# Two places for the turned probabilities of a background attention, and its output product moved behind the state's own products

## The reference

```python
x = x + _L0_ffn_ref(_layernorm(x), ...)      # causal attention, 16 heads of 64, then a mixture of 8 experts
x = x + _L1_xcond_ref(_layernorm(x), ctx_1024, cond_1024, ...)
# _L0_ffn_ref
q, k = l2norm(q) * q_scale, l2norm(k) * k_scale
logits = where(causal, einsum('bhid,bhjd->bhij', q, k) * 10, -1e9)
out = einsum('bhij,bhjd->bhid', softmax(logits), v).reshape(B, S, H * DH) @ Wo
h = layernorm(out, ln_g, ln_b)
# gate = softmax(h @ gate_w + gate_b); moe = sum over experts of gate * (gelu(h @ w1 + b1) @ w2 + b2)
# _L1_xcond_ref: 512 steps over the tokens
def step(h, x_t):
    attn = softmax(enc_hiddens . (h @ W))          # 77 keys
    context = attn . enc_hiddens
    # z, r, candidate of a GRU from [x_t, context] and h
    return z * h + (1 - z) * cand
```

## Time and profile before

| | us |
|---|---|
| median of 3 runs | 3392.69 (3389.45 to 3431.45) |
| profiled execution, its own time | 3399.51 |
| span of the profile | 3397.6 |
| mean granted TensorE clock | 0.937 of full |
| TensorE busy | 2864.2 (84%) |
| VectorE busy | 2216.0 (65%) |
| ScalarE busy | 1736.5 (51%) |
| GpSimd busy | 883.5 (26%) |

### The profile page before, as it was taken

The page is one execution under the profiler, slowest core; times in us unless marked ns, Lnnn a source line. Parts: engine busy times, 40 slices in busy tenths (PEclk is TensorE's granted clock), DMA queues, the critical chain, the costliest instruction groups (busy, mean ns, idle before and its releaser), DMA issues. The chain is left out here.

```text
span 3397.6 us, 132510 instructions
## 1 busy us (share of the span) xinstructions
PE 2864.2 (84%) x54702; PEld 1897.3 (56%) x54702; DVE 2216.0 (65%) x8486; ACT 1736.5 (51%) x5855; POOL 883.5 (26%) x1882
## 2 busy tenths in 40 slices
PE   5999999776987888898888899899989877777678
PEld 3666666653554454465454566566656544444478
DVE  4666666754426656677566677777768766666665
ACT  3666666433633444475555476666657433333222
POOL 0000000210002444254555344655535200000000
PEclk8999999987888878899899999999999999999879
DMA  4000000000010000010000000000000000000001
GB/s 130 4 5 7 5 4 4 1 10 9 16 51 9 9 9 27 3 40 4 9 9 27 4 28 16 7 10 10 25 10 28 4 3 3 3 4 3 2 32 32
DMA packets 35640, 52.45 MB, mean 15 GB/s; under 512 B 5406, under 2 KB 22760, under 8 KB 34920
## 3 DMA queue, kind: packets, MB, share of 16 engines
q1 hardware_dynamic: 34280, 41.54, 3.9%
q0 software_dynamic: 768, 2.52, 0.3%
HBM read 40.48 MB, written 3.57 MB: 13 GB/s over the span
## 5 line engine op out<-in xcount | busy, mean ns | idle before, releaser
L2010 POOL TENSOR_TENSOR gru_terms<-gru_states,gru_signs 128x8 f32<-128x8 f32 x512 | 103.5, 202 | 1573.7 <-DVE gru_states L2216 1245.0
L1931 ACT ACTIVATE gru_p<-gru_ps_sg,gru_negmax 128x78 f32<-128x78 f32 x512 | 166.9, 326 | 379.1 <-DVE gru_negmax L2185 374.0
L1774 PE MATMUL gru_ps_sg<-score_w,gru_states 128*4 128x78 f32 x4096 | 168.3, 237 | 194.7 <-DVE gru_states L2216 194.5
L1935 ACT ACTIVATE gru_th_r<-gru_pre_r 128x32 f32<-128x32 f32 x512 | 118.4, 231 | 398.6 <-DVE gru_pre_r L2196 398.6
L1572 PE MATMUL gru_ps_sg<-ctx_gate_w,gru_p_t 128*4 128x64 f32 x12288 | 281.1, 228 | 0.0
L342 ACT ACTIVATE self_probs<-self_sc,self_negmax 128x512 f32<-128x512 f32 x256 | 174.2, 684 | 166.2 <-DVE self_negmax L396 166.2
L1987 POOL TENSOR_SCALAR bg_probs<-bg_probs,bg_arsum 128x256 f32<-128x256 f32 (+2 forms) x192 | 240.5, 1253 | 19.0
L2205 DVE TENSOR_TENSOR_SCAN gru_c_in<-gru_th_r,gru_own 128x64 f32<-128x64 f32 x512 | 152.1, 297 | 123.3 <-ACT gru_th_r L1935 123.3
L1778 PE MATMUL gru_ps_own<-late,gru_states 128*4 128x128 f32 x4096 | 216.9, 285 | 0.0
L2185 DVE TENSOR_REDUCE gru_negmax<-gru_ps_sg 128x1 f32<-128x78 f32 x512 | 121.9, 238 | 141.0 <-PE gru_ps_sg L1774 135.6
L2196 DVE SCALAR_TENSOR_TENSOR gru_pre_r<-gru_ps_sg,gru_rtotal,gru_own 128x32 f32<-128x32 f32 x512 | 127.1, 248 | 129.1 <-PE gru_ps_sg L1572 118.9
(11 more groups left out here) (386 smaller groups left out, 7426.8 us busy)
## 6 DMA issues: line engine op xcount, KB each, us to landing
bg_w<-in_moe_w SPq DMA_DIRECT2D x48, 256.0 KB, 3.0
bg_wa<-in_wqkv SPq DMA_DIRECT2D x24, 192.0 KB, 2.3
moe_w<-in_moe_w SPq DMA_DIRECT2D x16, 256.0 KB, 2.9
picked_w_sb<-in_ec_w SPq DMA_DIRECT2D x16, 256.0 KB, 2.9
cross_scratch<-ctab_raw SPq DMA_DIRECT2D x16, 154.0 KB
late<-in_late SPq DMA_DIRECT2D x1, 2397.5 KB
cross_outs<-cross_scratch POOLq DMA_DIRECT2D x4, 576.0 KB, 6.2
self_w_sb<-in_wqkv SPq DMA_DIRECT2D x8, 192.0 KB, 2.3
```

Of the source, the lines that this page charges most:

```text
L1774: last = pe.matmul(ps_s[32 * b:32 * b + B, 0:CTX + 1], state(t), score_w[:, b, 0:CTX + 1], start=False, stop=True, tile_position=(0, 32 * ...
L1931: act.activation(p[:, 0:CTX + 1], ps_s[:, 0:CTX + 1], ACT.Exp, bias=negmax[:, 0:1], accum_out=total[:, 0:1])\
```

## The change

Turned probabilities of odd units go, at pace 2, to two places of `u`; those of even units and of pace 3 stay in `hid`. The copy waits for the values product two units back in place of one. The output product at pace 2 moves on TensorE from `before_scores`, where step t + 1 of the program runs it ahead of the unit's scores, to the end of `after_own` of step t. The first chunk of a tile's experts waits for all values products of the tile, since it writes `u`.

```diff
-        probs_t = hid
+        def turned_probs(g, m):
+
+            return u[:, 0:2, :] if PACE[g] == 2 and m % 2 else hid[:]
@@ values
-                        last = pe.matmul(bk_out[half, 0:P], v, probs_t[:, j, kt * P:(kt + 1) * P], start=kt == 0, stop=kt == g,
+                        last = pe.matmul(bk_out[half, 0:P], v, turned_probs(g, m)[:, j, kt * P:(kt + 1) * P], start=kt == 0, stop=kt == g,
@@ after_own
+                for g, n, m in units_at(t, "out"):
+                    if PACE[g] == 2:
+                        project_out(g, n, m)
+                        busy = True
                 if not busy:
@@ before_scores
                 for g, n, m in units_at(t, "out"):
-                    project_out(g, n, m)
-                    busy = True
+                    if PACE[g] == 3:
+                        project_out(g, n, m)
+                        busy = True
@@ unit_input
+                if n == 0:
+                    act.wait_ge(s_val, g * U)
@@ take_turned
-                wait_positive(act, s_val, m)
+                wait_positive(act, s_val, m - 1 if PACE[g] == 2 else m)
-                act.activation(probs_t[:, j, 0:(g + 1) * P], bk_turn[:, 0:(g + 1) * P], ACT.Copy).then_inc(s_apte, 1)
+                act.activation(turned_probs(g, m)[:, j, 0:(g + 1) * P], bk_turn[:, 0:(g + 1) * P], ACT.Copy).then_inc(s_apte, 1)
```

## The result

The changed kernel takes 3287.48 us (median of 4 runs, 3286.33 to 3287.84). The ratio to the kernel before is 0.963, 95% interval 0.955 to 0.972: faster. The span of the profiled execution is 3285.7 us in place of 3397.6.

A forecast was written before the change was run, and what follows sets the result against it. Bound: the recurrence chain at pace 2, 180 us of excess from even steps' copy wait and TensorE's clock. Gains 56 (g = 1) + 42.6 (g = 2) - 4 for drops give 95 us, 3298 from the median; range 3264 to 3345.

The forecast's parts named there:

- stretches: Steps 8 to 72 and 122 to 184, attention at pace 2: 336.3 and 326.9 us would become 280.3 and 280.4.
- two places, at full clock: Even steps: ScalarE's copy no longer waits for the values product; 1.66 us less at g = 1, 1.87 at g = 2.
- moved product: Odd steps: TensorE holds for ScalarE's output copy ahead of the sums; 0.86 us more on the chain, 3.77 to 4.63.
- clock: TensorE's granted clock, 0.81 and 0.92 in the stretches, would return to full; 4 us left for remaining drops.
- pair of steps, g = 1 / g = 2: An even and an odd step at pace 2 would take 8.64 us at g = 1, 8.92 at g = 2.
- 4 us left for drops: Both stretches: 4 us of the gain set aside for drops of TensorE's clock that remain.
- Clock stays: Rival: TensorE's new pause in odd steps replaces the old one, clock not recovered; 37 us more, 3335 us; chance 0.13.
- Short hold: Rival: output copy meets TensorE without pause, only the product's 0.41 us counts; 29 us less, 3269 us; chance 0.10.
- long hold: Rival: TensorE goes on only behind ScalarE's exponential L1861 in odd steps; 28 us more, 3326 us; chance 0.10.
- Slower: Rival: copy stays tied, even steps keep 5.67 us, odd ones pay 0.86; 55 us on top, 3448 us; chance 0.05.
- weight loads done ahead: TensorE, odd steps: sums' weight loads done during the hold might return 0.1 us a step, 6 us in all: 3292.

The follow-up runs named there:

- filled kernel: Kernel before plus ten unread filler products on TensorE behind the mask product of each even step of pace 2: 3346.30 us, ratio 0.976.
- filled move: Kernel before with the output product moved, one place for the turned probabilities, and ten filler products in even steps of pace 2: 3395.53 us, ratio 0.991.
- move with one place: Changed kernel with turned probabilities kept in one place, so only the output product is moved against the kernel before: 3495.15 us, ratio 1.022.

## Why the prediction was right

Forecast 3298 us, measured 3287.5. Each term below is measured by two kernels that differ in it alone, in us of the two stretches; those for the two places differ in the fillers too, which by their steps cost nothing:

| term | forecast | measured |
|---|---|---|
| two places, at full clock | 31 x 1.66 and about 31 x 1.8: 107 | 612.9 to 504.3: 108.6 |
| moved product | 64 x 0.86: 55 | 504.3 to 555.7: 51.4 |
| clock | as the sum has it, 32 + 15 less 4: 43 | 663.2 to 612.9: 50.3 |
| all three, 107 - 55 + 43 | 95 | 107.5 |
| pair of steps, g = 1 / g = 2 | 8.64 / 8.92 | 8.53 / 8.82 |
| stretches | 280.3 and 280.4 | 276.36 and 279.30 |

Every term was a little too pessimistic, so they did not cancel: from the profiled execution the sum promised 95 us and 112 came (3399.5 to 3287.5), 4 of them outside the stretches. That the forecast is only 10 us off has some luck in it: it was taken from the median, 3392.69, and not from the 3399.5 of the profiled execution that the rows come from, which put it 6.8 us nearer.

*Two places.* Right: the copy is hidden and TensorE ends the even step. I took 0.22 us from the mask product to the scores from the earlier trace rows, but there the scores waited for the state, which was done at 1110.71; where the state is already there, they follow the mask product by 0.13 us. That is 0.1 us a pair and some 6 us over both stretches, of which the last units, whose even steps were shorter already (4.75 to 5.4 us in the filled kernel), took most back. The split between the steps of a pair is also another one for g = 2 (3.91 and 4.91 for 4.29 and 4.63): I had counted TensorE's lateness in the step that causes it, and in the states it shows in the next.

*The moved product.* Right in place, cause and size: the hold lasts to 0.05 us behind the copy, the product takes 0.42 us, and the sums come 0.86 us later. The odd steps of the last four units are shorter (4.34 us), since no squares stand ahead of the copy there, which I had not counted; 64 full holds were a little too many. The prediction had the product 1.1 us earlier in its step; it starts 0.6 us earlier (1101.15 - 1099.27, for 1109.27 - 1106.76), and nothing hung on it. TensorE no longer waits for the weight load, 1.8 us before.

*The clock.* Recovered, as forecast, but its part was sized too small. The prediction also had two prices for it: the rival's 37 us has 10 for g = 2, while the sum, which took full-clock steps from a stretch at 0.92, has 15 there. Measured are 32.7 us for g = 1 and 17.7 for g = 2, and nothing of the 4 us left for drops. The reason given for the recovery was weaker than it looked. The prediction says that the pair's own 78% went with drops, but in the earlier trace rows the pair that was busy 78% had full clock, and the pair at 0.84 was busy 82%: the slower clock also makes the work longer, 8.56 us in place of 7.38 for the same 188 matmuls. Over whole stretches, the kernel before was busy 82% at 0.81 and the filled move 83% at 1.00. So a busy share alone does not tell the clock here. What the runs show is what went with it: with the even steps' pause of up to 1.9 us the clock fell, with that pause gone or filled it stood at 0.99 to 1.00, and the new pause of 0.67 us did not bring drops by itself.

*The rivals.* Clock stays: excluded by 0.99. Short hold and long hold: the sums follow the copy, in three kernels. Slower: the case of the copy that stays tied was built as the move with one place; at equal clock it costs 49 us where the prediction said 55, and with the clock 62. A hold decides against the change if it costs more than the even step gives; with the clock fixed the gain was 108.6 and the cost 51.4, so the change stood at half of that point.

*Order on TensorE.* Behind the held product the sums and then the gate products start at 1101.57 and 1101.87, in the order of the program. The Trainium skill, "TensorE: Matmul & The Clock Gate", says so of matmuls in Part 3, The mechanism; the trace agrees. The 0.1 us that weight loads done ahead might have given is not seen: the sums follow the product by the 0.42 us after which another matmul followed it before (0.41).

*What released the clock.* With fillers alone 0.81 and 0.92 became 0.99 and 1.00. The rule of the Trainium skill that activity releases the throttle ("TensorE: Matmul & The Clock Gate", Part 1, What's actually happening) agrees with that.

## What to carry to other kernels

A change of two parts can win with one and lose with the other: price each by itself at the place where its engine stands, and run them apart. An instruction moved to an earlier place takes its wait along. Here it cost the time from where its engine got there to the end of what it waited for, plus its own (0.86 us), and less (0.56 us) once part of what was queued behind it went ahead. A pause of TensorE that is repeated in each iteration can be paid a second time in its clock, as the one of up to 1.9 us was here and the one of 0.67 us by itself was not; when the wait itself can't go yet, fillers in it can get that part back.

## What the runs showed of the hardware

The kernel before scatters between 3390 and 3439 us on one chip, and the time goes with the clock granted over the span: 3390.24 at 0.940, 3433.38 at 0.927, 3438.94 at 0.923. With ten fillers per pair of steps the same program stays within 3345.1 to 3347.0, at 0.963 or 0.964 in all four runs. So nearly the whole scatter was the clock's; why a run gets the higher or the lower clock stays open. That fillers, which compute nothing of use, make a tuned kernel 2.4% faster than its median was more than I had expected.
